# Adding a token's two routed results on VectorE instead of GpSimd, in an attention and mixture-of-experts layer

## The reference

```
x  = x + layernorm(attention(layernorm(x)))
h  = layernorm(x)
logits = sigmoid(h @ gate_w + gate_b)          # 16 experts
values, experts = top_k(logits, 2);  values /= sum(values)
expert e of h:  (silu(h @ wg[e]) * (h @ wu[e])) @ wd[e]
ffn = h + shared(h) + values[0] * expert_0(h) + values[1] * expert_1(h)
x  = x + layernorm(ffn)
```

## Time and profile before

| | us |
|---|---|
| median of 3 runs (lowest to highest) | 2477.29 (2472.16 to 2482.36) |
| the profiled execution | 2484.09 |
| its span in the trace | 2482.3 |
| PE busy | 2305.1 (93%) |
| PEld busy | 1505.2 (61%) |
| DVE busy | 1978.6 (80%) |
| ACT busy | 1420.5 (57%) |
| POOL busy | 1679.4 (68%) |

### The profile page before, as it was taken

The page is one execution under the profiler, slowest core; times in us unless marked ns, Lnnn a source line. Parts: engine busy times, 40 slices in busy tenths (PEclk is TensorE's granted clock), DMA queues, the critical chain, the costliest instruction groups (busy, mean ns, idle before and its releaser), DMA issues.

```text
span 2482.3 us, 58247 instructions
## 1 busy us (share of the span) xinstructions
PE 2305.1 (93%) x18042; PEld 1505.2 (61%) x18042; DVE 1978.6 (80%) x5145; ACT 1420.5 (57%) x3248; POOL 1679.4 (68%) x2888
## 2 busy tenths in 40 slices
PE   4999999999999999999999999998889999999987
PEld 2555555555555555555555555564768888777754
DVE  5788888888888888888888888886555555888878
ACT  1465566665666665566655666655544555555544
POOL 2557667766777767677667777674567776777766
PEclk7899999999999999999999999998999999999998
DMA  4446544456544555444455444551444576667767
GB/s 130 132 118 167 147 129 137 134 154 162 156 132 135 155 152 168 121 131 121 143 143 146 132 129 135 144 152 49 146 146 152 166 215 217 215 220 233 234 204 243
DMA packets 300623, 387.59 MB, mean 156 GB/s; under 512 B 27872, under 2 KB 254176, under 8 KB 300192
## 3 DMA queue, kind: packets, MB, share of 16 engines
q1 hardware_dynamic: 274304, 312.52, 44.2%
q0 software_dynamic: 26016, 71.34, 7.9%
HBM read 193.14 MB, written 172.26 MB: 147 GB/s over the span
## 4 chain that ended last, share of the span: by engine, by line
PE 36%; POOL 32%; DMA 10%; issue 9%; DVE 8%; SPq 2%; ACT 1%; POOLq 0%; ACTq 0%; DVEq 0%
PE bank L1614 8%; DMA qs<-q_stack_dram 7%; PE ps_d L836 5%; PE bank L1628 4%; POOL q_parts L648 4%; POOL rest L650 4%; DMA k_stack_dram<-k_parts_negmax_t 3%; PE ps_d L843 3%; PE ps_d L790 3%; POOL sorted_dram L719 3%; POOL guess L688 2%; POOL k_parts_negmax_t L648 2%; POOL q_parts L650 2%; PE bank L1595 2%; POOL heads L730 2%
## 5 line engine op out<-in xcount | busy, mean ns | idle before, releaser
L933 ACT ACTIVATE probs<-ps_a 128x512 f32<-128x512 f32 (+1 forms) x1408 | 719.0, 558 | 482.5 <-PE ps_a L808 469.4
L1055 DVE TENSOR_REDUCE negmax<-ps_d 128x2 f32<-128x768 f32 (+3 forms) x768 | 778.4, 1032 | 130.3 <-PE ps_d L792 127.4
L790 PE MATMUL ps_d<-ks,qs 96*128 96x128 bf16 (+3 forms) x2048 | 490.5, 306 | 98.8 <-DMA qs<-q_stack_dram 66.5
L806 PE MATMUL ps_a<-qs,ks 99*128 99x512 bf16 (+3 forms) x2048 | 521.9, 303 | 9.9 <-ACT probs L933 7.0
L792 PE MATMUL ps_d<-mask_max,ident_bf 128*128 128x128 bf16 x2048 | 398.2, 223 | 0.0
L808 PE MATMUL ps_a<-mask_exp,ident_bf 128*128 128x128 bf16 x2048 | 390.5, 220 | 0.0
L790 PEld LDWEIGHTS ps_d<-ks,qs 96*128 96x128 bf16 x2048 | 203.3, 100 | 268.4 <-DMA qs<-q_stack_dram 76.5
L1525 POOL DMA_INDIRECT y_dram<-ysb,to_row x286 | 284.8, 996 | 100.5 <-POOL pool_cell L252 81.9
L820 PE MATMUL ps_out<-probs,va 128*32 128x512 f32 (+3 forms) x4096 | 330.5, 441 | 1.1 <-DVE by_token L1098 1.1
L806 PEld LDWEIGHTS ps_a<-qs,ks 99*128 99x128 bf16 x2048 | 199.5, 98 | 204.7 <-issue 62.2
L719 POOL DMA_INDIRECT sorted_dram<-h,slot x256 | 255.8, 999 | 66.3 <-issue 65.3
(11 more groups left out here) (206 smaller groups left out, 4374.3 us busy)
## 6 DMA issues: line engine op xcount, KB each, us to landing
qs<-q_stack_dram SPq DMA_DIRECT2D x128, 384.0 KB, 6.8
rows<-sorted_dram SPq DMA_DIRECT2D x286, 129.0 KB
y_in<-y_dram SPq DMA_DIRECT2D x32, 1024.0 KB, 6.4
q_stack_dram<-q_parts SPq DMA_DIRECT2D x64, 384.0 KB, 2.6
x_in<-in_x SPq DMA_DIRECT2D x32, 512.0 KB, 10.2
q_stack_dram<-q_parts SPq DMA_DIRECT2D x64, 256.0 KB, 2.9
x<-in_x SPq DMA_DIRECT2D x32, 512.0 KB, 4.8
h_dram<-h SPq DMA_DIRECT2D x32, 512.0 KB
```

The lines of the kernel that those rows point to most:

```text
L790: pe.matmul(ps_d[:, number % 2, at:at + width], qs[0:KR, b % 2, h, j * P:(j + 1) * P], ks[0:KR, b % 2, g, 0:width], start=True, stop=False)
L806: pe.matmul(ps_a[:, number % 3, at:at + width], ks[0:KM, b % 2, g, j * P:(j + 1) * P], qs[0:KM, b % 2, g * HG + h0 + k, j * P:T], start=Tr ...
L933: act.activation(probs[:, at:at + nh * width], ps_a[:, number % 3, 0:nh * width], ACT.Exp) \
L1055: dve.tensor_reduce(negmax[:, g // 2, j, at:at + nh], src, AX_X, ALU.max, negate=True) \
```

## The change

GpSimd's pair sum and its semaphore are gone. VectorE's `add_shared` adds each half of the shared sum, out of PSUM, to the first of the two routed results (before: to the pair sum), and then, over the whole sequence, adds the second routed result in a third instruction, both inputs of which lie in SBUF. A wait on `half_added` lies between. The waits for `y_loaded` and `finished` go from GpSimd to VectorE. `load_y` now waits for `s_added` (the end of VectorE's third addition) and, in the turns, is issued one sequence later.

```diff
--- before.py
+++ after.py
@@ -1391,7 +1391,7 @@
         s_turned, s_turned_out = sem("s_turned"), sem("s_turned_out")
         s_gate_done, s_up_done, s_gated, s_hid_ready = (
             sem("s_gate_done"), sem("s_up_done"), sem("s_gated"), sem("s_hid_ready"))
-        s_done, pair_added, s_added = sem("s_done"), sem("pair_added"), sem("s_added")
+        s_done, half_added, s_added = sem("s_done"), sem("half_added"), sem("s_added")
         stats_done, moments_done, root_steps, norm_ready = (
             sem("stats_done"), sem("moments_done"), sem("root_steps2"), sem("norm_ready"))
         x1_back, finished = sem("x1_back_ready"), sem("finished")
@@ -1468,7 +1468,7 @@
                 for k in range(YD):
                     sp.wait_ge(y_stored[k], 16 * stores_of(TILES[0] if b == 0 else ALL_TILES, k))
             if b >= NY:
-                sp.wait_ge(pair_added, b - NY + 1)
+                sp.wait_ge(s_added, b - NY + 1)
             sp.dma_start(y_in[:, b % NY], y_dram[2 * T * b:2 * T * (b + 1), :]
                          .rearrange("(j p k) d -> p j (k d)", p=P, k=2)).then_inc(y_loaded[b % NY], 16)
 
@@ -1492,8 +1492,8 @@
                     if b >= 3:
                         store(b - 3)
                         load_h2(b - 2 + NH - 1)
-                if i == 1 and b + NY < EARLY_FINALS:
-                    load_y(b + NY)
+                if i == 1 and 1 <= b < EARLY_FINALS - NY + 1:
+                    load_y(b + NY - 1)
 
         def rest():
             for b in range(EARLY_FINALS, EARLY_FINALS + NY):
@@ -1526,13 +1526,6 @@
                 out=y_dram[:, :], in_=ysb[:, k, :], in_offset=None,
                 out_offset=bass.IndirectOffsetOnAxis(ap=to_row[k][:, 0:1].bitcast(U32), axis=0),
             ).then_inc(y_stored[k], 16)
-
-        def add_pair(b):
-            pool.wait_ge(y_loaded[b % NY], 16 * (b // NY + 1))
-            if b >= NS:
-                pool.wait_ge(finished, b - NS + 1)
-            pool.tensor_tensor(summed[:, b % NS], y_in[:, b % NY, :, 0, :], y_in[:, b % NY, :, 1, :], ALU.add) \
-                .then_inc(pair_added, 1)
 
         def root(b):
             steps = Steps(pool, root_steps, 7)
@@ -1569,8 +1562,6 @@
             if 3 <= t < ALL_TILES + 3:
                 store_y(t - 3)
             for b, i in final_steps(t):
-                if i == 0:
-                    add_pair(b)
                 if i == 1 and b >= 1:
                     root(b - 1)
 
@@ -1579,8 +1570,6 @@
             for b in range(EARLY_FINALS, B + 2):
                 if b - 2 >= EARLY_FINALS:
                     root(b - 2)
-                if b < B:
-                    add_pair(b)
 
         return prepare, turn, rest
 
@@ -1857,13 +1846,17 @@
             dve.tensor_tensor(s_hid[:, :], bank_u(b)[:, :], s_gate[:, b % 2, :], ALU.mult).then_inc(s_hid_ready, 1)
 
         def add_shared(b):
+            dve.wait_ge(y_loaded[b % NY], 16 * (b // NY + 1))
+            if b >= NS:
+                dve.wait_ge(finished, b - NS + 1)
             dve.wait_ge(s_done, b + 1)
-            dve.wait_ge(pair_added, b + 1)
             for i in range(2):
                 halves = slice(2 * i, 2 * i + 2)
                 ps = bank_y(b, i)[:, :].rearrange("p (j d) -> p j d", j=2)
-                ins = dve.tensor_tensor(summed[:, b % NS, halves], ps, summed[:, b % NS, halves], ALU.add)
-            ins.then_inc(s_added, 1)
+                dve.tensor_tensor(summed[:, b % NS, halves], ps, y_in[:, b % NY, halves, 0, :], ALU.add) \
+                    .then_inc(half_added, 1)
+            dve.wait_ge(half_added, 2 * (b + 1))
+            dve.tensor_tensor(summed[:, b % NS], summed[:, b % NS], y_in[:, b % NY, :, 1, :], ALU.add).then_inc(s_added, 1)
 
         def gather(b):
             dve.wait_ge(s_added, b + 1)
```

## The result

| | before | after |
|---|---|---|
| median of 4 runs, us | 2477.39 | 2499.36 |
| lowest to highest | 2472.16 to 2482.36 | 2492.32 to 2502.93 |
| the profiled execution | 2484.09 | 2492.32 |

The ratio is 1.0087, with a 95% interval of 1.0061 to 1.0113: slower by 22.0 us. The forecast was 2496.5.

The account below looks back on a forecast made before the run. TensorE was taken to bound the overlapped stage, TensorE and VectorE both near the limit in the tail. 13.4 - 2.8 + 0 + 8.6 = +19.2 us gave 2496.5 us against the median of 2477.29; range 2480 to 2509.

Parts of the forecast that it names:

- The addition, 1.25 in the chain: VectorE's queue: the new 128x1024 addition takes 1.21 us plus 0.04 of wait, 1.25 us a sequence.
- Overlapped stage, 13.4 - 2.8 = +10.6: 2080 to 2365 us: `hid` is late, TensorE waits 0.79 us in 17 sequences, +13.4; 2.8 us comes back.
- What comes back, -2.8: Overlapped stage: TensorE's idle time on `hid_t` from ScalarE's `x_back`, late because GpSimd's root is late, returns 2.8 us.
- either go away or absorb: Overlapped stage: the 2.8 us of TensorE waits vanish or absorb as much of the new wait, -2.8 both ways.
- Stalls of `final` hidden in the turns: Overlapped stage: four `final` take 4.46 us instead of 1.66, but removing this 2.8 us stall returns nothing.
- SyncE at zero: SyncE's queue: the y load moved by one sequence makes its queue wait no more; VectorE's y wait also costs zero.
- Between the stages, 0: 2365 to 2398 us: a turning up to 1.25 later and ScalarE's copies freed of a late root together cost 0.
- Tail, +8.6: 2398.4 to 2468.6 us: VectorE's loop becomes 5.82 + 1.25 = 7.07 a sequence against 6.38 on average, +8.6 us.
- The loop over y: Tail: y loads issued behind `final`'s store arrive late and stretch the cadence from 6.04 to 6.38; the edit removes this.
- The slowed last projection: End of the tail: the last projection takes 2.98 in place of 1.99, 1.0 us kept in the forecast.
- The end at zero: Behind the tail's last sum: nothing changes, 13.7 us.
- Rival 3, the port: Overlapped stage: GpSimd's indirect DMAs stall the addition 0.34 to 1.0 in each of 17 sequences, +6 to +17; chance 0.13.

Follow-up runs that it names:

- pair ahead: Changed kernel, but VectorE adds the two routed results first, behind `finish`, and the halves then add to that sum; 2539.04 us beside 2540.72 for before, ratio 1.0011.
- loads only: Kernel before with only SyncE's part changed: y loads wait for `s_added`, one sequence later; 2541.24 us, late part 394.3 against 393.5.
- both: Kernel before with tail y loads ahead of the store, and VectorE adding the first 20 sequences' pairs behind `final`; 2525.53 us beside 2532.53, ratio 0.9972.
- y first: Kernel before with one edit: in the tail SyncE issues the y load ahead of the store and h2 load; 2531.08 us beside 2532.53, ratio 0.9989.
- GpSimd kept: Changed kernel, with GpSimd still making its pair sum into a buffer nobody reads; 2577.17 us, late part 435.4 against 415.0 for the changed kernel.
- half addition: Changed kernel with the third addition over only the first half of each sequence; 2541.73 us, late part 397.9 against 415.0 for the changed kernel.

## Why the prediction was right

It was right in sign, in size and in place; the whole of +19.2 was +21.5 in the profiles and +22.0 in the medians. By its steps:

- *The addition, 1.25 in the chain.* 1.225 and 0.03 for the wait. The row at half the elements and the one at 1024 were the right bounds.
- *Overlapped stage, 13.4 - 2.8 = +10.6.* Measured +10.8. The 17 waits are there, by 0.64 as recorded. The cadence grew by more, from 15.84 to 16.69 = 0.85 (0.79 was predicted): behind the wait, `hid`'s matmul takes 0.33 for 0.27 and the next ones start later as well. 17 x 0.85 = 14.4, of which 3.6 are absorbed.
- *What comes back, -2.8.* The size holds, the cause in part. I gave TensorE's waits on `hid_t` to GpSimd's late root. With the pair ahead on VectorE, ScalarE's waits for the root are gone (10.6 us in 15 waits before, none then), and TensorE's waits ahead of the tiles' down projection fall from 2.4 us in 7 to 0.7 in one. The overlapped stretch falls by 2.5 against "loads only", and in "both" by 2.4 against "y first", each pair from one chip; by 0.7 and 1.1 against the first profile of before. That much goes away with the late root. But the weight loads of that projection still wait in "pair ahead" as in before, and no longer after; before, pair ahead, after:

```profile
PEld bank L1628 <- issue: 9.1, 27, 1.0
...
PEld bank L1617 <- issue: 8.6, 31, 1.1
...
PEld bank L1617 <- issue: 0.6, 2, 0.5
```

  This part isn't the root's. `x_back`'s own time in ScalarE's queue may cause it; no run took that away. In the change it is absorbed, since TensorE waits on `hid` already. So "either go away or absorb" came out as something of both, which makes the 3.6.
- *Stalls of `final` hidden in the turns.* Shown by "GpSimd kept": 1.7 us.
- *SyncE at zero.* Shown by "loads only".
- *Between the stages, 0.* Measured -0.2, in part by luck: one cadence there has its clock at 0.76 in before and after alike, and where it stayed at 1.00 the same cadence is 3.5 us shorter. The prediction read this drop off rows 2, but priced it for the tail alone.
- *Tail, +8.6.* Measured +9.7, from cadences of 7.17 and not 7.07: from the start of `s_hid` to the sum it takes 2.84 (2457.42 to 2460.26) where I had 0.66 + 2.09. The loop over y is gone, as said. The slowed last projection stayed (8.17).
- *The end at zero.* A slip: the last sequence has the addition on its path as well, with nothing beside it. 14.9 against 13.7, +1.2.
- *Rival 3, the port.* Not there: 32 additions within 4 ns. What I took from one `kept_row` falls. An indirect DMA of GpSimd next to `final` in the profile after, VectorE's line and then GpSimd's:

```profile
2349.25 1.66 DVE L1879 SCALAR_TENSOR_TENSOR final<-summed,rstd,x_back 128x256 f32<-128x256 f32 x4
...
2349.26 0.98 POOL L1525 DMA_INDIRECT y_dram<-ysb,to_row  x1 [0.46 <-POOL pool_cell L252]
```

The four take 1.66 as ever. In the profile after, 68 of the 128 `final` and 4 of the 32 additions lie beside an indirect DMA, and none is longer for it. The Trainium skill ("SBUF — State Buffer", section "Who interferes with whom") has it that a `tensor_tensor` takes only the read interface of the shared pair and that descriptor generation needs the write interface, which it marks as inferred, and that a GpSimd instruction that reads SBUF contends with two SBUF inputs. The trace agrees with both: 0.483 is the longest `final` beside descriptor writing, 2.65 the longest addition beside GpSimd's sum in "GpSimd kept". `kept_row` was held from 2336.99, 0.37 before the recorded start of GpSimd's sum at 2337.36. It isn't alone: sixteen `final` of before, 0.48 long otherwise, start 0.5 to 0.6 before that recorded start and end 0.3 after the sum's end. So it was more likely the sum that held it, from before its recorded start, than the DMA; a run that parts the two wasn't made.

## What to carry to other kernels

An instruction moved to an engine with idle time is paid for by its place in that engine's queue: ask what the bounding engine fetches next behind it, and how many tenths of a us there are in hand. Here 1.25 us with 0.41 in hand cost 0.85 in each of 17 sequences, while stalls of 2.8 us, one step further on in the same queue, had cost nothing. When an engine waits for a load, look first at what stands before that load in the queue that issues it: the order of two lines on SyncE was worth 4.3 us in the tail, where the pair sum on VectorE, at its better place, cost 2.1.

## What the runs showed of the hardware

- One execution's front part differs by 13 us from another's with the same instructions, by up to 20 between profiles of one chip, and by 37 to 57 between the first profile of before and those of this section. The last 400 us of the changed kernel repeat within 1. Stretches with the same code in "y first" and before differ by 1.3, and by 3.1 where the clock fell in one of them. A change in a late stage is better read there than in the total, and with the clock beside it.
- The same 26 matmuls took 9.87 us at a granted clock of 0.76 and 6.80 at 1.00.
- A 128x1024 float32 addition takes 1.225 on VectorE and 2.36 on GpSimd. Over 512 elements it takes 0.693 on VectorE ("half addition"). The halves, with PSUM and SBUF inputs, cost 0.680 before and 0.686 after; "y first", with the tiles of before, has 0.686 too.
- A recorded wait of 0.64 on TensorE cost 0.85: the first matmuls behind it are spread out too, and the busy time of the stage grows (273.8 of 285 us after, 271.2 of 274 before) with nothing more to do.
